# Expert layer L3_FFN: ranks and shares of the next unit within the unit in front, their spread by ScalarE at the unit's end, the result's norm later

## What is computed

```
# x: [256,128] of one unit; w_gate [16,128]; 16 experts of 64 hidden units, one shared pair of 128
scores  = sigmoid(x @ w_gate.T)                      # 16 scores in 4 groups of 4
group_scores = sum of the two best of each group
allowed = the two groups with the best group_scores  # ties: lower index wins
idx     = the 4 best experts within them;  w = scores[idx] / (sum + 1e-6)
combine = one_hot(idx) * w, summed                   # [256,16], the "shares"
g = silu(x @ w1_e.T);  u = x @ w3_e.T                # all 16 experts, dense
routed = einsum('tef,ehf,te->th', g * u, w2_e, combine)
shared = silu(x @ w1_s.T) * (x @ w3_s.T) @ w2_s.T
x = x + layernorm(routed + shared)
```

## Time and profile before

| | us |
|---|---|
| median of 3 runs | 1428.1 (1427.24 to 1428.37) |
| the profiled execution | 1429.44, span 1427.6 |
| PE busy | 1166.2 (82% of the span) |
| DVE busy | 1044.9 (73%) |
| ACT busy | 727.0 (51%) |
| POOL busy | 423.7 (30%) |
| L3_FFN by itself (from the first `gated` of unit 0) | 1288.4 to the end |

### The profile page before, as it was taken

How to read it: one execution, slowest core, us unless ns; L and a number is a source line. 1 busy time by engine, 2 the same in 40 slices (tenths; PEclk the granted TensorE clock), 3 DMA queues, 4 the chain that set the end, 5 groups by cost and what they waited for, 6 DMA issues and landing times.

```text
span 1427.6 us, 27186 instructions
## 1 busy us (share of the span) xinstructions
PE 1166.2 (82%) x9362; PEld 835.4 (59%) x9362; DVE 1044.9 (73%) x2899; ACT 727.0 (51%) x1186; POOL 423.7 (30%) x639
## 2 busy tenths in 40 slices
PE   5989898999987777758677878687779888888887
PEld 3666667888863333337444444576667445557776
DVE  7888875666666777736778998778886676768886
ACT  4445433333334666646476777443434566654442
POOL 5545441000033342212545554213122233201110
PEclk9999998999995999978798999798899899999999
DMA  8000000000000000000000000000000000000001
GB/s 344 1 1 1 1 1 0 0 0 0 0 1 1 1 1 0 1 1 1 1 1 1 0 1 2 1 1 1 1 1 2 1 3 0 2 2 1 1 1 30
DMA packets 5846, 14.64 MB, mean 10 GB/s; under 512 B 240, under 2 KB 4464, under 8 KB 5360
## 3 DMA queue, kind: packets, MB, share of 16 engines
q1 hardware_dynamic: 5744, 13.33, 2.5%
HBM read 12.28 MB, written 1.05 MB: 9 GB/s over the span
## 4 chain that ended last, share of the span: by engine, by line
issue 33%; PE 30%; DVE 18%; DVEq 6%; POOLq 5%; ACT 5%; POOL 4%; ACTq 0%
PE PS L1899 5%; PE PS L1908 3%; PE PS L1290 2%; PE PS L1203 2%; PE PS L1118 2%; POOL trs L416 2%; PE PS L1095 2%; PE PS L1487 1%; DVE w_l0f L2421 1%; PE PS L1224 1%; PE PS L1117 1%; PE PS L1230 1%; DVE sbuf L2089 1%; DVE h L1961 1%; DVE mx L2182 1%
## 5 line engine op out<-in xcount | busy, mean ns | idle before, releaser
L2182 DVE TENSOR_REDUCE mx<-PS 128x2 f32<-128x512 f32 (+1 forms) x256 | 155.1, 620 | 73.7 <-PE PS L1234 32.9
L737 ACT ACTIVATE w_l0f<-PS 128x512 f32<-128x512 f32 (+1 forms) x256 | 136.8, 543 | 96.1 <-PE PS L1241 46.7
L414 POOL TENSOR_TENSOR tve<-tmv,eps 128x2 f32<-128x2 f32 x64 | 14.7, 229 | 496.4 <-DVE tmv L1970 297.2
L1899 PE MATMUL PS<-hT_padded,w_l0f 128*128 128x256 f32 x512 | 122.2, 385 | 0.0
L1899 PEld LDWEIGHTS PS<-hT_padded,w_l0f 128*128 128x128 f32 x512 | 94.7, 194 | 11.0
L1027 ACT ACTIVATE sg<-PS 128x512 f32<-128x512 f32 x64 | 38.2, 597 | 120.3 <-PE PS L1899 120.3
L1658 PE MATMUL PS<-w_l2f,y 128*128 128x128 f32 x512 | 75.8, 295 | 18.7 <-ACT y L900 9.5
L1658 PEld LDWEIGHTS PS<-w_l2f,y 128*128 128x128 f32 x512 | 71.3, 208 | 26.7 <-ACT y L900 16.3
L2421 DVE SCALAR_TENSOR_TENSOR w_l0f<-w_l0f 128x768 f32<-128x768 f32 x64 | 67.5, 1055 | 17.8 <-ACT w_l0f L812 16.5
L3083 DVE TENSOR_TENSOR y<-sg,PS 128x512 f32<-128x512 f32 x64 | 43.9, 687 | 49.9 <-ACT sg L1027 42.6
L1908 PE MATMUL PS<-w_l0f,y 128*128 128x128 f32 x512 | 69.0, 278 | 6.1 <-DVE y L3083 6.1
(11 more groups left out here) (499 smaller groups left out, 3309.5 us busy)
## 6 DMA issues: line engine op xcount, KB each, us to landing
w_l0f<-in_l0f SPq DMA_DIRECT2D x1, 3076.0 KB, 17.7
w_l2f<-in_l2f SPq DMA_DIRECT2D x1, 2214.0 KB, 18.8
w_l3f<-in_l3f SPq DMA_DIRECT2D x1, 1736.0 KB, 22.6
w_l0a<-in_l0a SPq DMA_DIRECT2D x1, 960.0 KB, 7.6
result<-X SPq DMA_DIRECT2D x1, 896.0 KB, 4.6
X<-in_x SPq DMA_DIRECT2D x1, 768.0 KB, 10.9
PT<-in_cbf SPq DMA_DIRECT2D x1, 640.0 KB, 8.7
w_l1f<-in_l1f SPq DMA_DIRECT2D x1, 582.0 KB, 14.8
```

What stands on the lines that cost most here:

```text
L737: act.activation(P8[:, hh % 8, 0:width], PS[:, hh % 2, 0:width], ACT.Exp, scale=SM_SCALE).then_inc(a["pt"], 1)
L1899: ins = pe.matmul(PS[:, 2 * (c % 2) + g, b * L:(b + 1) * L], w("l0f", "w1")[:, at:at + P], hT[:], start=True, stop=True)
L2182: dve.tensor_reduce(mx[:, hh, 0:nm], PS[:, 2 + hh % 2, 0:nm * keys].rearrange("p (t k) -> p t k", t=nm), AX.X, ALU.max).then_inc(a["mx"], 1)
```

## The change

ACT: `spread(i)` stood behind `gate(i, 0)`, inside unit i. It now stands behind `gate(i - 1, 4)`, the last gate of the unit in front, and ahead of `gate_exp(i + 1)` and of `gate(i, 0)`. Only unit 0's stays where it was.

DVE: in slots 2 to 4 the ranking of the experts is moved up. `greater` and `ties` go from slot 3 to slot 2, `beaten` and `ranked` from slot 4 to slot 3, and `chosen` to `shares` from the end of the unit to the end of slot 3, ahead of `logits` and of `gated(i, 4)`. The result's statistics go from slot 2 to slot 3; its norm and its sum stay in slot 4 with `gated(i, 4)` in front of them. No instruction is added or taken away but drains: a unit that has all three kinds of side work has twelve of them from `gated(i, 2)` on, where it had nine.

```diff
--- before.py
+++ after.py
@@ -969,8 +969,10 @@
                     for i in range(NB):
                         for c in range(LAST_CHUNKS):
                             gate(i, c)
-                            if c == 0:
-                                spread(i)
+                            if i == 0 and c == 0:
+                                spread(0)
+                            if c == 4 and there(i + 1):
+                                spread(i + 1)
                             if c == 1 and there(i - 1):
                                 result_copy(i - 1)
                             if c == 3 and there(i + 2):
@@ -2888,37 +2890,26 @@
                             below_the_rest()
 
                         gated(i, 2)
+                        dve.drain()
+                        shared_out(i, 2)
+                        if G:
+                            equal(msk[:], E16)
+                            greater(msk[:], E16)
+                            dve.drain()
+                            ties("rank16", E16)
+
+                        gated(i, 3)
+                        dve.drain()
+                        if G:
+                            beaten(E16)
+                        shared_out(i, 3)
                         if D_:
                             result_stats(i - 1)
-                        dve.drain()
-                        shared_out(i, 2)
-                        if D_:
-                            result_moments()
-                        if G:
-                            equal(msk[:], E16)
-
-                        gated(i, 3)
-                        if G:
-                            greater(msk[:], E16)
-                        dve.drain()
-                        shared_out(i, 3)
-                        if G:
-                            ties("rank16", E16)
-
-                        if S:
-                            logits(s)
-                        gated(i, 4)
-                        dve.drain()
-                        if G:
-                            beaten(E16)
-                        shared_out(i, 4)
-                        if D_:
-                            result_norm(i - 1)
                         dve.drain()
                         if G:
                             ranked(rank[:], E16)
                         if D_:
-                            result_add(i - 1)
+                            result_moments()
                         dve.drain()
                         if G:
                             chosen()
@@ -2930,6 +2921,17 @@
                             share_inverse()
                             dve.drain()
                             shares()
+                        if S:
+                            logits(s)
+
+                        gated(i, 4)
+                        dve.drain()
+                        shared_out(i, 4)
+                        if D_:
+                            result_norm(i - 1)
+                            dve.drain()
+                            result_add(i - 1)
+                        dve.drain()
                     result_stats(NB - 1)
                     dve.drain()
                     result_moments()
```

## The result

The changed kernel takes 1443.84 us in the median of 4 runs (1441.51 to 1444.89) against 1428.23 of before (1427.24 to 1429.62): ratio 1.0101, 95% interval 1.0073 to 1.0129. It is slower by 15.6 us; the forecast was 13.1 slower. The profiled execution has a span of 1441.0 us, 13.4 above that of before.

A forecast was written before the change was run, and what follows sets the result against it. VectorE was taken to set the pace before, and ScalarE's 5.29 us chain behind the shares after. Unit 0 +2.55, units 1 to 5 +10.93, unit 6 +0.1, unit 7 -0.5: +13.1 on 1428.1 gives 1441 us, range 1437 to 1446.

The forecast's parts named there:

- VectorE sets the pace before, TensorE's wait for `PT` is slack: Last layer before the change: VectorE works back to back, 17.12 us a unit; TensorE's 2.05 us wait is slack.
- ScalarE's chain, 5.29 us, wait 2.8: From `cwn`'s end to the next unit's first gated product: spread, loads, exponential, gate take 5.29 us; VectorE waits 2.8.
- Unit 0, +2.55: Unit 0, with no result to normalise: the next unit starts at 19.04 us, 2.55 us more.
- Units 1 to 5, +10.93: Five units at a period of 19.68 us, 98.40 us against 87.47, 10.93 us more.
- Unit 6, +0.1: Unit 6, no state work or loads: VectorE's and ScalarE's ends come out alike, near 16.0 us; +0.1, -0.4 to +0.4 around it.
- Unit 7, -0.5: Last unit, paced by TensorE: `PT` is ready long before `down(6, 4)` is over, saving 0.5 us.
- What I gave a chance of 0.2: Slow-clock rival: longer TensorE waits bring an uncovered slow stretch in unit 7, 1.6 to 3 us; 1442.7 to 1444 us.
- The slow stretches within units 1 to 5: TensorE at a low granted clock mid-layer: VectorE's wait for ScalarE leaves room, so nothing was counted.
- The price of a table switch: ScalarE table load: 1.29 to 1.30 us by the trace; rival with the skill's 2.66 us gives 1457.5, chance 0.03.
- The rival 'VectorE's pace', 1423.7: ScalarE's chain runs beside the wait for shares, VectorE's order sets 16.94 us a unit: -4.4 us, 1423.7; chance 0.05.
- The rival 'no effect', 1458: Something holds `cwn` back, so the spread starts where it did; ScalarE is 2.8 us later a border: 1458; chance 0.02.

The follow-up runs named there:

- VectorE's order alone: Changed kernel with ScalarE's part undone, so spread(i) is again behind gate(i, 0): 1427.48 us against 1427.73, ratio 0.9993.
- The second trace: The changed kernel measured once more with nothing altered: 1440.51 us against 1428.11, ratio 1.0095.
- ScalarE's order alone: Kernel before with only ScalarE's part of the change, spread(i + 1) behind gate(i, 4): 1461.53 us, ratio 1.0231.
- the kernel without table loads: Changed kernel with Silu in place of Exp for the routing of units 2 to 7: 1429.47 us against 1428.58, ratio 1.0001.
- the kernel with the later router's product: Kernel before with only `logits` moved behind shared_out(i, 4) on VectorE: 1425.44 us, ratio 0.9986; again 1423.19 us, ratio 0.9966.

## Why the prediction was right, point by point

- *VectorE sets the pace before, TensorE's wait for `PT` is slack*: right. With the wait gone nothing is gained; with the wait left and VectorE's own wait gone, 16.5 us a unit.
- *ScalarE's chain, 5.29 us, wait 2.8*: right. 5.30 and 2.83, and it shrinks with each piece that is taken out of it.
- *Unit 0, +2.55*: +2.64 (19.13 against 16.49).
- *Units 1 to 5, +10.93*: +12.15. The period worked out as 19.68 is 19.78 in three of them, since `cwn` came 0.09 us later than priced (14.29 against 14.20), and 20.13 and 20.14 in the two others. Each of these two has one wait that is put down to issue: 0.45 us in front of L2284 in unit 1, 0.43 in front of L2242 in unit 3. The kernel before has waits of that kind too (0.43 in unit 6); what causes them I didn't try to find out.
- *Unit 6, +0.1*: +0.3.
- *Unit 7, -0.5*: this is the step that failed. It is +1.1 (20.35 against 19.27). The working behind it holds: VectorE's order alone has 18.7 there, 0.6 less than before. What I gave a chance of 0.2 happened in both traces of the changed kernel: a slow stretch of 1.7 us that nothing covers. My reason for it, the longer waits of the new order near a border, is not shown: among the kernels with VectorE's new order, the wait in front of these matmuls is 1.98 us in those with the stretch and in those without.
- *The slow stretches within units 1 to 5*: right, they are covered. The changed kernel has three, at the `up` behind the wait for `shared_out` (3.57, 2.89 and 2.56 us for eight matmuls instead of 1.99), at the ends of units 1, 2 and 3. Unit 2 is 19.78 us all the same, as long as units 4 and 5, which have none. The second trace has them at the same three places (3.46, 2.78 and 2.44 us) and the same lengths of units.
- *The price of a table switch*: the Trainium skill (ScalarE: Activation LUTs, What ACT_TABLE_LOAD costs) gives 2.66 us for each switch, a drain included. By that figure the wait would be 5.6 us and the time 1457.5, both estimates. The trace does not agree: each load is again 1.28 with 0.01 to 0.02 behind it, and the wait is 2.83. The trace decides for the rows, by which I had forecast 1441.
- Together the layer took 16.2 us more in the profiled pair and 13.1 were worked out. The medians are 15.6 and, in the second measurement, 12.4 apart, and the spans 13.4; they hold the scatter of what lies ahead of the layer, 2.8 us in the pair of spans. That the second median, 1440.5, falls on the forecast is therefore luck: its layer is as long as the first one's.
- *The rival 'VectorE's pace', 1423.7*: its price was wrong, as the run of that order alone showed: 1427.5. The three drains cost what I had counted (0.15 each), but 0.17 more a unit, the small waits in three units and 0.63 behind unit 0 ate the rest of the gain.
- *The rival 'no effect', 1458*, a spread that starts no sooner with the loads behind it: ScalarE's order alone is that case, and it took 1461.5.

## What to carry to other kernels

Before a step is moved ahead on an in-order engine, add up what stood ahead of it at its new place and now stands behind it, up to the next instruction that another engine waits for: here 3.3 us of loads, exponential and gate against 2.8 us by which the data came sooner. Table switches belong where the engine idles anyway, here ahead of the wait for the shares, and a switch back could be forced there with a one-element activation (0.20 us). And the wait that is largest on TensorE (17 us at `PT`) was pure slack, while 0.6 us a unit on the engine without other gaps was worth moving one instruction.

## What the runs showed of the hardware that I had not expected

TensorE's slow stretches come and go between kernels, and what starts them is not shown here. The wait in front of unit 7's `up` was 1.98 us where the eight matmuls took 3.03 us, at a granted clock of 0.65 from 1419.50 to 1424.40 (a mix of the levels 1.2 and 2.4 GHz), and in the kernel without table loads, where they took 3.68, and in VectorE's order alone, where they took 1.99. Unit 6 of the kernel with the later router's product has such a stretch in both of its traces, and before had none there. Such a stretch costs 1.5 to 1.7 us where no other wait covers it; the best reordering here brought 2.3 and 4.9 us in its two measurements. The start of the last layer differs by up to 6.2 us between traces, though the instructions up to there are the same, and that is more than this gain.
